# Graph and expert layer on one core: where the key blocks start, when the edge lists load, and which engine makes small tables

## The reference

```
xn = layernorm(x)
gnn:  h[r, n] = mean over edges e of relation r into n of xn[src_e] * w_e
      gnn = sum_r h[r] @ weight[r] + xn @ root + bias
mix:  q, k, v = xn @ wq + bq, xn @ wk + bk, xn @ wv + bv;   q, k -> elu + 1
      kv = k^T v per head;  k_sum = sum k;  mix = (q kv) / (q k_sum + 1e-6) @ wo + bo
x = x + gnn + mix
ffn:  router = softmax(relu(f @ r1 + b1) @ r2 + b2), best two of 6 experts
      expert e: relu(relu(f @ w1 + b) @ w2 + b) @ w3 + b, summed with the two weights
out = x + ffn(layernorm(x))
```

## Time and profile before

| what | us |
|---|---|
| median of 3 runs (3027.4 to 3027.52) | 3027.47 |
| the profiled execution, its own time | 3028.82 |
| its span | 3027.3 |
| last product of stage A, first of stage B | 617.5, 630.15 |
| first products of the loop | about 891 |
| one iteration of the loop | 87.6 |

### The profile page before, as it was taken

The page is one execution under the profiler, slowest core; times in us unless marked ns, Lnnn a source line. Parts: engine busy times, 40 slices in busy tenths (PEclk is TensorE's granted clock), DMA queues, the critical chain, the costliest instruction groups (busy, mean ns, idle before and its releaser), DMA issues.

```text
span 3027.3 us, 47261 instructions
## 1 busy us (share of the span) xinstructions
PE 2934.1 (97%) x16707; PEld 2567.4 (85%) x16708; DVE 2189.2 (72%) x5317; ACT 1765.7 (58%) x3392; POOL 1659.3 (55%) x1700
## 2 busy tenths in 40 slices
PE   6999999969989999999999999999999999999998
PEld 5888878858778888888888888888888888888887
DVE  4479664125668787778888777788777778878775
ACT  3555555523446665666666566666666566666555
POOL 1000000042257777777777777777777777777740
PEclk9999999989999999999999999999999999999999
DMA  7677677875443444444444444443444444344420
GB/s 258 249 267 272 261 276 269 292 250 174 146 140 107 129 131 132 133 127 129 118 121 133 133 134 129 131 122 118 134 131 131 134 126 129 116 128 131 131 74 11
DMA packets 182224, 473.45 MB, mean 156 GB/s; under 512 B 46934, under 2 KB 105260, under 8 KB 159747
## 3 DMA queue, kind: packets, MB, share of 16 engines
q0 software_dynamic: 80544, 221.54, 25.4%
q1 hardware_dynamic: 99248, 247.02, 22.6%
q10 hardware_dynamic: 2196, 1.86, 0.2%
HBM read 312.80 MB, written 158.29 MB: 156 GB/s over the span
## 4 chain that ended last, share of the span: by engine, by line
PE 68%; DVE 6%; ACT 2%; DVEq 1%; issue 1%; DMA 1%; SPq 0%; ACTq 0%
PE bank L1647 45%; PE acc L1704 8%; PE acc L1710 8%; PE acc L1647 2%; DVE sel L1362 2%; PE bank L1674 1%; PE bank L1810 1%; DVE x L1457 1%; PE bank L1683 1%; PE bank L1693 1%; DVE stats_c L1461 1%; PE bank L1760 1%; DVEq L1459 1%; DVE h_lo L1487 1%; ACT h_hi L1205 1%
## 5 line engine op out<-in xcount | busy, mean ns | idle before, releaser
L1135 POOL DMA_INDIRECT ring<-y_tab,tab x1666 | 1642.6, 986 | 653.4 <-issue 497.5
L1205 ACT ACTIVATE h_hi<-bank,bias_t 128x512 fp32r<-128x512 f32 (+1 forms) x600 | 407.7, 679 | 315.6 <-PE bank L1647 280.1
L1487 DVE TENSOR_TENSOR h_lo<-bank,h_hi 128x512 fp32r<-128x512 f32 (+1 forms) x600 | 382.1, 675 | 228.1 <-ACT bank L1206 226.2
L769 PE MATMUL yb<-wr_hi,xhl 128*128 128x512 f32 x1568 | 509.4, 402 | 14.5 <-ACT yst L350 12.5
L1192 ACT ACTIVATE row_hi<-ring,tab 128x256 fp32r<-128x256 f32 x1091 | 449.6, 497 | 14.4 <-PE acc L1710 13.5
L1379 DVE SCALAR_TENSOR_TENSOR row_lo<-ring,tab,row_hi 128x256 fp32r<-128x256 f32 x1091 | 447.8, 478 | 7.8 <-ACT row_hi L1192 7.8
L350 ACT ACTIVATE yst<-yb 128x512 f32<-128x512 f32 x392 | 229.8, 596 | 273.6 <-PE yb L769 245.5
L1206 ACT ACTIVATE bank<-bank,bias_t 128x512 f32<-128x512 f32 (+1 forms) x600 | 386.3, 644 | 0.0
L769 PEld LDWEIGHTS yb<-wr_hi,xhl 128*128 128x128 f32 x1568 | 298.6, 190 | 88.8 <-ACT yst L350 15.2
L1647 PE MATMUL bank<-ew_hi,h_hi 128*128 128x256 f32 x1176 | 342.7, 291 | 1.5 <-DVE h_lo L1487 1.4
L1647 PE MATMUL bank<-ew_lo,h_hi 128*128 128x256 f32 x1176 | 329.1, 280 | 0.0
(11 more groups left out here) (265 smaller groups left out, 5514.7 us busy)
## 6 DMA issues: line engine op xcount, KB each, us to landing
y_tab<-yst SPq DMA_DIRECT2D x97, 1024.0 KB, 4.1
ring<-y_tab,tab POOLq DMA_INDIRECT x1666, 2.8
xt_tab<-xhl SPq DMA_DIRECT2D x25, 1024.0 KB, 4.6
xk<-xt_tab SPq DMA_DIRECT2D x25, 1024.0 KB, 4.9
xc<-xt_tab SPq DMA_DIRECT2D x25, 1024.0 KB, 5.4
x<-x_tab SPq DMA_DIRECT2D x49, 256.0 KB, 3.2
xs<-in_x SPq DMA_DIRECT2D x24, 512.0 KB, 6.0
x_tab<-xs SPq DMA_DIRECT2D x24, 512.0 KB, 5.0
```

The costliest lines, as they stand in the source:

```text
L769: last = pe.matmul(out_ap, a, b, start=(i == 0), stop=(i == len(parts) - 1))
L1135: pool.indirect_dma_start(out=out_ap, out_offset=None, in_=y_tab[:, :], in_offset=bass.IndirectOffsetOnAxis(ap=idx_ap, axis=0)).then_inc(s ...
L1205: act.activation(dest[:, m, 0:W], b[:, 0:W], ACT.Relu, bias=bias)
L1487: gone(dve.tensor_tensor(lo_[:, m, 0:W], bank[plan[kind, (e, m)][0]][:, 0:W], hi[:, m, 0:W].bitcast(F32), ALU.subtract))
```

## The change

- The transposed features of groups 23 and 24 stay in SBUF after stage A (`xhl` lives on and is the keys' `xk`), and the key blocks begin with these six; group d is loaded when its buffer is read out. The loads of expert weights move behind the loads of groups 2 and 6.
- The edge lists load at tiles 0, 2, 4 and 8 with a semaphore each; the copies to `dpad` move from tiles 5 and 6 to 11 and 12.
- In the key portions 5 to 8, `high` goes two rows at a time over the second to fourth block, `low_rows` one row at a time from the sixth block to the last.
- `tables` and the spreading copy move from DVE to ACT. Tables 0 and 1 are made by ACT ahead of the first key block, and wait for both table loads; the copy stands behind `gate_t` at expert 1, and before the loop behind the copy of `kw`.
- `sel` reads its row of numbers from `ramp`, which lies in PSUM, instead of `iota_w` in SBUF.

```
-                    if u < 4:
-                        a, into = ((dst, lin_d), (etype, lin_t), (src, lin_s), (ew, lin_w))[u]
-                        sp.dma_start(into[0:ROWS, :], by_row(a)).then_inc(lin_in, 16)
+                    if u in (0, 2, 4, 8):
+                        i = (0, 2, 4, 8).index(u)
+                        a, into = ((dst, lin_d), (etype, lin_t), (src, lin_s), (ew, lin_w))[i]
+                        sp.dma_start(into[0:ROWS, :], by_row(a)).then_inc(lin_in[i], 16)
...
+            KEPT = SUPER - 2
+            key_order = list(range(SUB * KEPT, TILES_N)) + list(range(SUB * KEPT))
+            def key_place(d):
+                return d % 2 if d >= KEPT else (d + SUPER) % 2
...
                 def load_xk(d):
-                    if d >= 2:
-                        sp.wait_ge(key_proj, SUB * (d - 1))
+                    sp.wait_ge(key_proj, SUB if d == 0 else SUB * d + LAST_T)
...
-                load_xk(0)
                 load_table(0)
...
-                load_xk(1)
                 load_table(1)
-                load_w(0, e_w1, 0)
-                sp.dma_start(stage_r[:, :, :], r_w1.rearrange("(k p) n -> p k n", p=P)).then_inc(w_in[0], 16)
-                load_w(1, e_w2, 1)
-                for d in range(2, SUPER):
+                for d in range(KEPT):
                     load_xk(d)
+                    if d == 2:
+                        load_w(0, e_w1, 0)
+                        sp.dma_start(stage_r[:, :, :], r_w1.rearrange("(k p) n -> p k n", p=P)).then_inc(w_in[0], 16)
+                    if d == 6:
+                        load_w(1, e_w2, 1)
...
+                def by_feature(i):
+                    act.wait_ge(rden_set, i + 2)
+                    act.activation(rden_c[:, :, :].rearrange("p t (h d) -> p (t h) d", h=HEADS),
+                                   rden[:, :, :].rearrange("p t h -> p (t h)").unsqueeze(2)
+                                   .to_broadcast([P, SUB * HEADS, C // HEADS]), ACT.Copy).then_inc(rden_ready, 1)
+                def tables(n):
+                    act.wait_ge(tab_in[n % 2], 16 * SUB * (n // 2 + 1))
+                    for t in range(SUB):
+                        last = act.activation(rel_w[:, n % 2, t, :], tab[:, n % 2, t, :, 1], ACT.Identity,
+                                              bias=neg_t[:, SUB * n + t:SUB * n + t + 1])
+                    last.then_inc(rel_set, 1)
...
+                        if more and e == 1:
+                            by_feature(i)
                         for p in SPLIT_AT.get(e, ()) if more else ():
                             high(i + 1, p)
+                        if more and e == EXPERTS - 3 and i + 2 < SUPER:
+                            tables(i + 2)
...
+                act.wait_ge(neg_set, 1)
+                tables(0)
+                tables(1)
...
-                            if p > PLAIN and j == 2:
-                                high(0, p - 1)
+                            if p > PLAIN and 1 <= j <= PT // 2:
+                                high(0, p - 1, range(2 * j - 2, 2 * j))
...
                         gone(act.activation(kw_sb[:, :, :], b[:, :].rearrange("p (k n) -> p k n", k=KC), ACT.Copy))
+                        by_feature(-1)
...
+                    dve.wait_ge(rel_set, n + 1)
                     tables_free(dve, n, p)
...
-                        last = dve.tensor_scalar(sel[:, p % BUFS, q, :], iota_w[:, :], rel_w[:, n % 2, t, k:k + 1],
+                        last = dve.tensor_scalar(sel[:, p % BUFS, q, :], ramp[:, 0:NT], rel_w[:, n % 2, t, k:k + 1],
...
-                            if p > PLAIN and j == 4:
-                                low_rows(0, p - 1)
+                            if p > PLAIN and j >= 5:
+                                low_rows(0, p - 1, range(j - 5, j - 4) if j < len(keys_of(p)) - 1 else range(j - 5, PT))
```

More of the change, by code:

```diff
@@ L104, in gps_layer @@
         eq = sbuf(whole, "eq", [P, KC, NS])
+        with ExitStack() as px:
+            xhl = sbuf(px, "xhl", [P, 2, 2, KC, NS], F32R)
+        w3_hi = sbuf(whole, "ew2_hi", [P, EXPERTS, KC, C], F32R)
+        qf = sbuf(whole, "qf", [P, KC, NS])
         pa = ExitStack()
@@ L186, in gps_layer @@
             wkv_hi_set, wkv_split = (sem(n) for n in ("wkv_hi_set", "wkv_split"))
-            wkv_in, wr_in, small_in, bkv_in, rows_in_e, lin_in = (
-                sem(n) for n in ("wkv_in", "wr_in", "small_in", "bkv_in", "rows_in_e", "lin_in"))
+            wkv_in, wr_in, small_in, bkv_in, rows_in_e = (
+                sem(n) for n in ("wkv_in", "wr_in", "small_in", "bkv_in", "rows_in_e"))
+            lin_in = [sem(f"lin_in{i}") for i in range(4)]
             pads_set, ident_set, consts_set, misc_full, misc_free = (
@@ L862, in gps_layer @@
             w_lo = [sbuf(pc, f"ew{i}_lo", [P, EXPERTS, KC, C], F32R) for i in range(2)]
[L863 to L865 removed]
+            w_hi.append(w3_hi)
+            xk = xhl
             w_lo.append(sbuf(pc, "ew2_lo", [P, EXPERTS, KC, C], F32R))
@@ L889, in gps_layer @@
             row_lo = sbuf(pc, "row_lo", [P, SLOTS, PT, C], F32R)
+            with ExitStack() as px:
+                ek = sbuf(px, "ek_c", [P, 2, C])
             xlo = sbuf(pc, "xlo", [P, C], F32R)
+            xsel = sbuf(pc, "xsel", [P, NT], F32R)
+            spare = sbuf(pc, "spare", [P, NT])
             with ExitStack() as px:
@@ L1183, in queries, with high @@
                         act.activation(b[:, 0:NS], b[:, 0:NS], ACT.Relu, bias=bias_t[:, BQ + m:BQ + m + 1]).then_inc(q_set, 1)
-                def high(n, p):
+                def by_feature(i):
[9 more added lines that the diff above has]
+                    last.then_inc(rel_set, 1)
+                def high(n, p, some=range(PT)):
                     if p >= parts(n):
                         return
[L1188 to L1191, removed]
+                    size = len(tiles_of_portion(p))
+                    if some[0] == 0:
+                        act.wait_ge(tab_in[n % 2], 16 * SUB * (n // 2 + 1))
+                        act.wait_ge(rows_in[p % SLOTS], 16 * gathers(n, p))
+                        tables_free(act, n, p)
+                    for q in range(some[0], min(some[-1] + 1, size)):
+                        t, k = tiles_of_portion(p)[q]
                         last = act.activation(row_hi[:, p % BUFS, q, :], ring[:, p % SLOTS, q, :],
                                               ACT.Copy, scale=tab[:, n % 2, t, k, 2:3])
-                    last.then_inc(hi_ready, 1)
+                    if some[-1] >= size - 1:
+                        last.then_inc(hi_ready, 1)
                 def iteration(i, plan):
@@ L1347, in attention @@
                         gone(dve.tensor_tensor(qf[:, k, :], qf[:, k, :], b[:, 0:NS], ALU.mult))
-                def tables(n):
-                    dve.wait_ge(tab_in[n % 2], 16 * SUB * (n // 2 + 1))
-                    for t in range(SUB):
-                        dve.tensor_scalar(rel_w[:, n % 2, t, :], tab[:, n % 2, t, :, 1], float(n * NS + t * NT), None,
-                                          ALU.subtract)
-                    dve.drain()
                 def weighted(n, p):
@@ L1372, in one_hot, with low_rows @@
                                       rel_w[:, n % 2, t, k:k + size].unsqueeze(2).to_broadcast([P, size, NT]), ALU.is_equal)
-                def low_rows(n, p):
+                def low_rows(n, p, some=range(PT)):
                     if p >= parts(n):
                         return
-                    dve.wait_ge(hi_ready, split_before(n, p) + 1)
-                    for q, (t, k) in enumerate(tiles_of_portion(p)):
+                    size = len(tiles_of_portion(p))
+                    if some[0] == 0:
+                        dve.wait_ge(hi_ready, split_before(n, p) + 1)
+                    for q in range(some[0], min(some[-1] + 1, size)):
+                        t, k = tiles_of_portion(p)[q]
                         last = dve.scalar_tensor_tensor(out=row_lo[:, p % SLOTS, q, :], in0=ring[:, p % SLOTS, q, :],
@@ L1382, in low_rows @@
                                                         op0=ALU.mult, op1=ALU.subtract)
-                    last.then_inc(lo_ready, 1)
+                    if some[0] < size <= some[-1] + 1:
+                        last.then_inc(lo_ready, 1)
                 def prepare(n, p):
@@ L1544, in iteration @@
                             low_rows(i + 1, p)
-                        if more and e == EXPERTS - 3:
-                            if i + 2 < SUPER:
-                                tables(i + 2)
                         if e == EXPERTS - 1:
@@ L1573, in _ @@
                 dve.memset(zv[:, :, :, :], 1.0)
-                tables(0)
+                dve.drain()
                 for p in range(PARTS):
@@ L1604, in _ @@
                                           ALU.subtract).then_inc(w_split_c, 1)
-                tables(1)
                 prepare(1, 0)
@@ L1816, in _ @@
                     for v in keys_of(p):
-                        if v % SUB == 0:
```

(4 more changed lines are left out.)

42 lines of the change are left out of this document (21 added, 21 removed).

## The result

The changed kernel takes 3037.79 us, median of 7 runs (3034.53 to 3040.66), against 3027.40 for the kernel before in the same session: ratio 1.0037, 95% interval 1.0026 to 1.0049, 8 to 15 us slower. Direction and range (3026 to 3062) held; the forecast of 3048.5 was 10.7 too high. This is not one term mis-sized by 10. The two loop terms came out near the forecast; the miss is mostly two gains, one in stage A that the prediction did not contain at all and one in the key portions, and smaller losses hide part of them.

The account below looks back on a forecast made before the run. PE, busy 97%, bounds the kernel; only its waits or half-clock stretches matter. Terms -8 -7 +1 +1.6 +19.1 +14.4 = +21.1 us on 3028.8 give 3049.9, less the profile's 1.35: 3048.5 us, range 3026 to 3062.

Parts of the forecast that it names:

- The two loop terms: In the loop: `sel` reading from PSUM, +19.1 us, and the spreading copy on ACT at expert 1, +14.4 us.
- Twelve `sel` from PSUM: Loop's end, ahead of `q1`: twelve `sel` take 3.99 us instead of 3.16, +0.83 per iteration, +19.1 us in all.
- the rows' slope: For `sel`: 1.02 ns per column from PSUM against 0.48 from SBUF, 69 ns more per `sel`, fixed part unchanged.
- rival 4: Loop's `sel`: a fixed PSUM cost of 0.065 us each comes on top, 18 us, total 3066; chance 0.05.
- The copy at expert 1: Loop: the spreading copy on ACT delays `h1(3,0)`; 0.35 us slack against 1.0 delay, 0.6 us 24 times, +14.4 us.
- Stage A's loads: Stage A: edge-list loads spread over tiles leave two stops, 8 us, of 15.7 lost; a gain of 8 us (0 to 15.7).
- Key start: First key blocks: first wait exchanged for nothing or a small loss, group 0's `xk` wait shortened; a gain of 7 us.
- The exchange of the first wait: First key block: no `xk` wait, but tables and their loads on ACT put the exp 1.5 us later.
- Before the loop: Ahead of the loop: the spreading copy on ACT delays `high(0, 11)`, DVE's `low_rows` and PE's closing sum, +1.6 us.
- The key portions: Key portions: spread splits save 4 us of stops, new waits cost 3.2, slower `sel` 1.6; sum +1 us (-3 to +3).
- the new waits: Key portions: about 1.2 us ahead of `aggregate` in portions 5 and 7, 0.8 in portion 8; +3.2 us.
- the slower `sel`: Key portions: 24 `sel` each slower by 0.07 us, with no slack, +1.6 us.

Follow-up runs that it names:

- ab_lin: a_both with the four edge-list loads again at the first four tiles: 3011.54 us, 0.9952 of the kernel before.
- ab_whole: a_both with the first group's `high` and `low_rows` again in one piece per portion: 3006.32 us, 0.9931 of the kernel before.
- a_sel: The changed kernel with `sel` reading its row of numbers from SBUF again: 3019.18 us, 0.9974 of the kernel before.
- b_pad: The kernel before with 32 unused bytes ahead of `xhl`, shifting it and what follows in stage A: 3018.49 us, 0.9970.
- b_place: The kernel before with the changed kernel's SBUF layout, instructions, waits and loads as before: 3013.80 us, 0.9955.
- a_both: The changed kernel with `sel` reading from SBUF and the spreading copy on DVE again: 3003.00 us, 0.9919 of the kernel before.

## Why the prediction was half right

Divide the two profiles at the same places, and each stretch has its own forecast:

| stretch | forecast, us | measured, us |
|---|---|---|
| to the end of the last `yb` product | -8 | -16.7 |
| to the eleventh `key_features` | -7 | -5.0 |
| to the last `key_features` | +1 | -5.5 |
| to the first `gate_t` | +1.6 | +1.6 |
| first to last `gate_t` | +33.5 | +36.6 |
| all, measured by the spans | +21.1 | +10.9 |

- **Twelve `sel` from PSUM**, +19.1: measured 16.8, and 0.75 in the iteration shown in place of 0.83. Right, the rows' slope 10% high. The mean of `sel` rose by 47 ns and its median in the timeline from 343 to 402, 59. Slope alone gave 69. By the Trainium skill, page "VectorE: DVE Perf Modes", section "The TRN2 errata — SBUF-src ops pay a fixed extra latency per instruction", the fixed part from PSUM is 62 cycles longer, an estimate of 65 ns, and 134 together with the slope. So the two do not come together, which was rival 4; but which of the two it is, one width cannot tell, and no run here had `sel` at another. The prediction's remark that the rows speak against the page is borne out only so far, that both do not add. (Rival 4's 0.065 us is the page's figure. The spread of the rows, 148 against 295 ns, does not give it.)
- **The copy at expert 1**, +14.4: measured 15.4. Slack and delay, read from one iteration, were right, and so was the instruction that pays.
- **Stage A's loads**, -8: 7.8 (ab_lin).
- **Key start**, -7: right. The exchange of the first wait is small and a loss: from the end of the last `yb` product to the first `key_features` product it takes 22.1 to 23.0 us in the five kernels with the old start and 24.0 to 25.5 in the eight with the new one, about 2 more where 1.5 was forecast. Group 0 gave back 6.4 of 7.76 us. To the eleventh `key_features` it is 55.7 to 58.1 us in the five and 48.4 to 50.7 in the eight, 7 less by the means; the pair of profiles in the table shows 5.0.
- **Before the loop**, +1.6: a wait of 1.10 on PE, and 1.6 more from the last `key_features` to the first `gate_t`.
- **The key portions**, +1: the step that failed among those named. The sum of stops removed (-4) against new waits (+3.2) had two sizes wrong: the new waits are 1.06 and 1.07 us, and the stop where the split of the weights falls was of 3.42 us in the kernel before and is 2.12 now. The spreading is worth 3.3 us by ab_whole's median and 3.8 by its profile, not clear of noise; that the rest of it is clock is argued from the granted clock of that profile (0.91 against 0.96). And the slower `sel` costs nothing here, where 1.6 was forecast: first to last `key_features` takes 208.3 in the changed kernel, 208.8 in a_sel.
- **The layout**, not in the prediction: 8 to 13 us by b_pad and b_place. The diff says that `xhl` moves; the prediction costed its instructions and waits and took a product's duration as given. This is the largest part of the miss of 10.7. Against b_place, which has the layout alone, the change costs 24.0 us (23.1 if each is taken against the kernel before beside it); the sum said 21.1. That these lie so close is in part luck: against b_place the key portions gained 2.5 where a loss of 1 was forecast, and the loop lost 3 more than forecast.

What is left: the loop of a_both is 4.1 longer than before, of which the place of `h1` and `h2` gives some 3 us (0.14 per iteration); single longer iterations come on top and are open. And the key blocks differ by 3.8 us between profiles of kernels that share them (222.3 in the kernel before, 218.5 in b_pad). A part of that is clock by the records: from 780 to 800 us the granted clock is 0.87 in the kernel before (part of it at 1.2 GHz) and 1.00 in b_pad. What sets it was not tested.

## What to carry to other kernels

On an engine that is busy 97%, check first whether its own pace changed: count the instructions in a stretch that the change doesn't touch. A diff that moves a tile in SBUF can change the pace of every product that reads it as weights, so cost the move, or try 32 bytes of padding, before you look for the cause in the schedule. Divide two profiles at the same places and hold each stretch against its own forecast: the total hid an error of 9 and one of 6. And where work is moved to another engine, follow what is queued behind it to the first instruction that the bounding engine waits for: slack against delay gave 14.4 where 15.4 was measured.

## What the runs showed of the hardware

A product of 128x512 whose weights come from a tile at a multiple of 64 bytes of the partition had a median of 396 to 397 ns in the profile, and 389 with the tile 32 bytes further (`xhl` stood at a multiple of 64 in three of these kernels and 32 past one in two places, with no exception; 96 past a multiple of 128 was not tried for it). For `h1` and `h2` a step of the same kind was 3 to 4 ns per product (397 against 393 and 394) and 0.14 us of an iteration of 87.7. A `sel` of 128 columns with its row of numbers in PSUM took 402 ns, from SBUF 343. Four loads of 781 KB each in a row beside stage A cost it 7.8 us more than the same four two to four tiles apart.
